# Second layer of a two-layer transformer block: the maxima's remainder on GpSimd, another order of the transposed scores, and a later copy of the attention outputs

## What is computed

```python
q, k, v = heads(xn @ Wq.T) * 8 ** -0.5, heads(xn @ Wk.T), heads(xn @ Wv.T)
sim = where(key > query, -max, q @ k.T)
e = exp(sim - max(sim, axis=-1))            # the maximum of each query's row
attn = (e @ v) / (sum(e) + 1e-8) @ Wo.T
moe = sum over 8 experts of (silu(xn @ wg) * (xn @ wu)) @ wd    # 128 -> 512 -> 128
x = x + attn + moe
```

## Time and profile before

| | us |
|---|---|
| three runs | 1370.39, 1373.32, 1380.13 (median 1373.32) |
| the profiled execution's time | 1372.09 |
| its span, first to last instruction | 1370.4 |
| PE busy | 1304.3 (95%) |
| DVE busy | 1017.8 (74%) |
| ACT busy | 823.6 (60%) |
| POOL busy | 738.1 (54%) |

### The profile page before, as it was taken

One profiled execution on the slowest core, in us unless ns is written; L12 is line 12 of the kernel. 1 busy time (PEld: TensorE's weight loads), 2 busy tenths in 40 slices (PEclk: granted clock), 3 DMA queues, 4 the chain that ended last, 5 costly groups with the idle time before them and its releaser, 6 DMA issues. The chain is left out here.

```text
span 1370.4 us, 23500 instructions
## 1 busy us (share of the span) xinstructions
PE 1304.3 (95%) x8328; PEld 779.8 (57%) x8328; DVE 1017.8 (74%) x2369; ACT 823.6 (60%) x1235; POOL 738.1 (54%) x859
## 2 busy tenths in 40 slices
PE   8999999999999969999999999999999999999996
PEld 5444545554455435665665665665665666666664
DVE  4676777777777647877887887787787788788764
ACT  2456666666766736666666666666566566566561
POOL 6154464664655535565655655655655654655551
PEclk9899999999999989999999999999999999999999
DMA  5222232423433311112112111111110110100002
GB/s 190 63 93 72 93 119 93 136 89 125 135 107 105 120 54 33 36 43 65 51 51 65 52 51 36 35 51 32 39 51 30 40 52 29 41 28 30 18 16 85
DMA packets 57683, 90.94 MB, mean 66 GB/s; under 512 B 12087, under 2 KB 23356, under 8 KB 57566
## 3 DMA queue, kind: packets, MB, share of 16 engines
q1 hardware_dynamic: 56414, 88.91, 20.5%
q10 hardware_dynamic: 1152, 0.52, 0.1%
HBM read 43.75 MB, written 44.53 MB: 64 GB/s over the span
## 5 line engine op out<-in xcount | busy, mean ns | idle before, releaser
L1261 POOL TENSOR_TENSOR a_h_lo<-a_h,a_h_hi 128x512 fp32r<-128x512 f32 x256 | 328.8, 1285 | 153.8 <-ACT a_h_hi L1333 153.2
L192 POOL TENSOR_SCALAR_AFFINE_SELECT E<-E 128x256 f32<-128x256 f32 (+1 forms) x384 | 195.1, 511 | 350.8 <-ACT E L1340 209.0
L701 DVE TENSOR_REDUCE mx<-bank_pair 128x2 f32<-128x1024 f32 (+3 forms) x264 | 209.5, 818 | 110.6 <-PE bank_pair L949 109.1
L1415 DVE SCALAR_TENSOR_TENSOR a_h<-a_h,bank_pair 128x512 f32<-128x512 f32 x256 | 175.2, 685 | 144.5 <-ACT a_h L1329 144.4
L1333 ACT ACTIVATE a_h_hi<-a_h 128x512 fp32r<-128x512 f32 x256 | 161.6, 631 | 128.4 <-DVE a_h L1421 125.6
L1340 ACT ACTIVATE E<-bank_pair 128x1024 f32<-128x1024 f32 (+1 forms) x192 | 169.6, 883 | 114.9 <-PE bank_pair L140 114.9
L168 DVE CUSTOM_DVE_ANT_0 bank_pair<-bank_pair,mask 128x512 f32<-128x512 f32 x496 | 230.6, 517 | 0.0
L133 PE MATMUL bank_pair<-st 24*128 24x512 f32 (+3 forms) x1024 | 200.1, 387 | 17.2 <-ACT E L789 3.5
L789 ACT ACTIVATE E<-bank_pair 128x1024 f32<-128x1024 f32 (+1 forms) x192 | 168.3, 878 | 70.3 <-PE bank_pair L140 68.8
L1421 DVE TENSOR_TENSOR a_h<-a_h,bank 128x512 f32<-128x512 f32 x256 | 176.1, 688 | 27.4 <-DVE a_h L1415 0.9
L1329 ACT ACTIVATE a_h<-bank_pair 128x512 f32<-128x512 f32 x256 | 151.1, 590 | 74.8 <-PE bank_pair L1556 73.4
(11 more groups left out here) (201 smaller groups left out, 2331.3 us busy)
## 6 DMA issues: line engine op xcount, KB each, us to landing
st<-stack_d SPq DMA_DIRECT2D x256, 96.0 KB
o_d<-O SPq DMA_DIRECT2D x64, 256.0 KB, 2.1
stack_d<-l_q_k_hi SPq DMA_DIRECT2D x56, 256.0 KB, 3.1
stack_d<-l_q_k_lo SPq DMA_DIRECT2D x28, 256.0 KB, 3.4
st<-ms SPq DMA_DIRECT2D x128, 8.0 KB
wst<-wg_in SPq DMA_DIRECT2D x8, 256.0 KB, 2.9
wst<-wu_in SPq DMA_DIRECT2D x8, 256.0 KB, 3.2
wst<-wd_in SPq DMA_DIRECT2D x8, 256.0 KB, 3.7
```

The lines of the kernel that those rows point to most:

```text
L192: return nc.gpsimd.affine_select(out=part, in_=part, compare_op=ALU.is_ge, fill=0.0, base=0, pattern=pattern, channel_multiplier=-1)
L701: ins = nc.vector.tensor_reduce(out, pair[:, :, col:col + width(kb)], AX.X, ALU.max)
L1261: nc.gpsimd.tensor_tensor(h_lo[:, q % RH, :], h[:, q % RH, :], h_hi[:, q % RH, :].bitcast(F32), ALU.subtract).then_inc(h_lo_ready, 1)
L1415: nc.vector.scalar_tensor_tensor(hq, hq, 1.0, g_bank[:, :], ALU.add, ALU.mult).then_inc(silu_ready, 1)
```

## The change

Five edits, all in `attend_moe`:

1. **The maxima's remainder.** `negations` goes. VectorE now writes the rounded maxima, not negated, with a `tensor_reduce` over an axis of length one (`tops`, slot 5). GpSimd subtracts that from the maxima (`rest_of_maxima`, 128x16 numbers, at the head of slot 6). The sign is put in by `copy_mrow` with `scale=-1.0`.
2. **Order of the transposed scores.** 0, 1, 3, 4, 5, 2 instead of 0 to 5 (`KEY_ORDER`), for the matmuls, the exponentials and the zeros.
3. **The copy of the outputs.** `outputs(g - 1)` moves on ScalarE from behind `hi` of slot 3 to slot 7, between `copy_mrow` and `hi`.
4. **Late units.** ("A", k) for k from 1 to 7 moves from quad 4k+1 to 4k+2; V of batch 6 goes to quad 5 and V of batch 7 to quad 9.
5. **SyncE.** The inverse's spreading load (`load_share`) is issued ahead of the outputs' store, not behind it.

```diff
+KEY_ORDER = (0, 1, 3, 4, 5, 2)
...
-LATE = {0: ("X", 6), 1: ("A", 0), 2: ("X", 7), 3: ("Q", 6), 4: ("K", 6), 5: ("A", 1), 6: ("V", 6), 7: ("Q", 7), 8: ("K", 7), 9: ("A", 2),
-        10: ("V", 7), 13: ("A", 3), 17: ("A", 4), 21: ("A", 5), 25: ("A", 6), 29: ("A", 7)}
+LATE = {0: ("X", 6), 1: ("A", 0), 2: ("X", 7), 3: ("Q", 6), 4: ("K", 6), 5: ("V", 6), 6: ("A", 1), 7: ("Q", 7), 8: ("K", 7), 9: ("V", 7),
+        10: ("A", 2), 14: ("A", 3), 18: ("A", 4), 22: ("A", 5), 26: ("A", 6), 30: ("A", 7)}
...
                 if due[0] == "A":
                     store_rden(due[1])
+                if due[0] == "A":
+                    load_share(due[1])
                 if g > 0:
                     sp.wait_ge(O_copied, g)
                     store_outputs(sp, o_d, O, g - 1, o_out[(g - 1) % 2])
-                if due[0] == "A":
-                    load_share(due[1])
                 if coming[0] == "A" and coming[1] > 0:
                     load_attention(coming[1])
...
+            def rest_of_maxima(g):
+                pool.wait_ge(top_ready, g)
+                nc.gpsimd.tensor_tensor(neg_part(nm, 1), mx[:, g % 2, :, :], neg_part(nm, 0).bitcast(F32), ALU.subtract).then_inc(nm_ready, 1)
...
                 for n in range(NC):
+                    if odd and n == 2 and g + 1 < QUADS:
+                        rest_of_maxima(g + 1)
                     if odd and n < 3:
                         causal(g, 3 + n)
...
-                nc.scalar.activation(ms[:, g % 2, :], M_bank[0:MAXIMA, :], ACT.Copy).then_inc(mrow_ready, 1)
+                nc.scalar.activation(ms[:, g % 2, :], M_bank[0:MAXIMA, :], ACT.Copy, scale=-1.0).then_inc(mrow_ready, 1)
...
                     if odd and n == NC - 1 and g + 1 < QUADS:
                         copy_mrow(g + 1)
+                    if odd and n == NC - 1 and g > 0:
+                        outputs(g - 1)
                     hi(NC * i + n)
...
-                    if not odd and n == NC - 1 and g > 0:
-                        outputs(g - 1)
...
-            def negations(g):
+            def tops(g):
                 dve.wait_ge(S_used, SCORES * g)
                 if g > 1:
                     dve.wait_ge(mT_ready, g - 1)
-                negate(nc, nm, mx, g).then_inc(neg_ready, 1)
-                dve.wait_ge(neg_ready, g)
-                negate_rest(nc, nm, mx, g).then_inc(nm_ready, 1)
+                nc.vector.tensor_reduce(neg_part(nm, 0), mx[:, g % 2, :, :].unsqueeze(3), AX.X, ALU.max).then_inc(top_ready, 1)
```

More of the change, by code:

```diff
@@ L1165, in attend_moe @@
         mrow_in = sem("mrow_in")
-        neg_ready, nm_ready, mT_ready, mrow_ready = (sem(n) for n in ("neg_ready", "nm_ready", "mT_ready", "mrow_ready"))
+        top_ready, nm_ready, mT_ready, mrow_ready = (sem(n) for n in ("top_ready", "nm_ready", "mT_ready", "mrow_ready"))
         S_ready, S_used, T_ready, exp_done = sem("S_ready"), sem("S_used"), sem("T_ready"), sem("exp_done")
@@ L1267, in split, with causal @@
                                         ALU.subtract).then_inc(w_lo_ready, 1)
-            def causal(g, n):
-                pool.wait_ge(exp_done, UNITS_A_QUAD * g + n + 1)
+            def causal(g, m):
+                n = KEY_ORDER[m]
+                pool.wait_ge(exp_done, UNITS_A_QUAD * g + m + 1)
                 keep_causal(nc, E[:, (PLANES * g + n // 3) % SLOTS_E, :], n % 3).then_inc(masked, 1)
+            def rest_of_maxima(g):
+                pool.wait_ge(top_ready, g)
+                nc.gpsimd.tensor_tensor(neg_part(nm, 1), mx[:, g % 2, :, :], neg_part(nm, 0).bitcast(F32), ALU.subtract).then_inc(nm_ready, 1)
             def rest_of_late(kind, b):
@@ L1333, in hi, with exp @@
                 nc.scalar.activation(h_hi[:, q % RH, :], h[:, q % RH, :], ACT.Copy).then_inc(h_hi_ready, 1)
-            def exp(g, n):
+            def exp(g, m):
+                n = KEY_ORDER[m]
                 at_col, w, pair = EXP_AT[n % 3], EXP_WIDTH[n % 3], PLANES * g + n // 3
-                act.wait_ge(T_ready, UNITS_A_QUAD * g + n + 1)
+                act.wait_ge(T_ready, UNITS_A_QUAD * g + m + 1)
                 if n % 3 == 0 and pair >= SLOTS_E:
@@ L1468, in _ @@
                     if more and odd and n == 1:
-                        negations(g + 1)
+                        tops(g + 1)
                     if odd and n == 2 and coming[0] == "A":
@@ L1495, in scores_and_keys @@
                 score_blocks = UNITS[n % 3] if more else []
-                key_blocks = UNITS[m % 3] if here else []
+                key_unit = KEY_ORDER[m] if here else 0
+                key_blocks = UNITS[key_unit % 3] if here else []
                 for k in range(2):
@@ L1506, in scores_and_keys @@
                         if k < len(key_blocks):
-                            ins = keys_by_queries(nc, T_banks[:, r, :], stacks[g % STACKS], r, m // 3, key_blocks[k])
+                            ins = keys_by_queries(nc, T_banks[:, r, :], stacks[g % STACKS], r, key_unit // 3, key_blocks[k])
                             if r == HALVES - 1 and k == len(key_blocks) - 1:
```

## The result

| | before | after |
|---|---|---|
| median, us | 1372.88 (4 runs) | 1400.31 (4 runs) |
| lowest to highest | 1370.39 to 1380.13 | 1398.22 to 1405.07 |
| ratio | | 1.0197, 95% interval 1.0162 to 1.0232 |
| profiled execution, span | 1372.09, 1370.4 | 1399.45, 1397.7 |
| mean granted clock of TensorE | 0.980 | 0.961 |

The account below looks back on a forecast made before the run. TensorE's queue was taken to set the time. From 1372.1 us, gains of 28.2 came off and 1 (SyncE's queue), 30.5 (wait at `invert`) and 7 (clock) were added: 1382 us, range 1361 to 1402.

Parts of the forecast that it names:

- The wait at `invert`: Slot 6, seven quads: VectorE waits for `den`, so TensorE stands 4.65 us each time, 30.5 us in all.
- The clock: TensorE's clock falls behind two of the seven stalls, 3.3 us a fall, taken as 7 us; bounds 0 and 23.
- I take 1 us in all: SyncE at the quad's end: the moved copy delays the maxima's rows, 1 us in all, bounds 0 and 6.
- The gain of 0.90 us a quad: Remainder and order: 0.36 + 0.10 + 0.34 + 0.10 us a quad, 28.2 us in all.
- slot 3 becomes like slot 1: Slot 3, new order: from scores to `down` 0.77 falls to 0.43 us, 0.34 us less a quad.
- VectorE must run earlier too. It can: Slots 4 and 5: with the copy gone from ahead of slot 4's `tanh`, VectorE's work moves up by 0.35 us.
- The remainder: Slot 5: the reduction runs unblocked at L180's price, 1.2 us less on VectorE, of which TensorE gains 0.36 + 0.10 a quad.
- the cover: GpSimd, slot 6: the subtraction is ready about 1 us before TensorE wants it in slot 7, so it costs nothing.
- (a): Rival: TensorE's clock falls at every stall, 23 us for the falls, 1398 us; chance 0.22.
- (b): Rival: VectorE eats the order's gain, only 14 us are won, 1397 us; chance 0.13.
- (c): Rival: more is won, 1.4 us a quad and no fall of the clock, 1358 us; chance 0.10.
- (d): Rival: the wait at `invert` does not bite and the change only gains, 1345 us; chance 0.05.

Follow-up runs that it names:

- f1: The changed kernel with the inversion of ("A", 1 to 7) moved to slot 1 of the quad LATE names: 1360.19 us, ratio to before 0.9903.
- f3: The changed kernel with both repairs, the inversion a quad later and the parts' stores ahead of SyncE's wait: 1343.36 us, ratio to before 0.9785.
- f2: The changed kernel with SyncE issuing the Q and K parts' stores ahead of its wait for the outputs' copy: 1387.74 us, ratio to before 1.0115.
- e7: The changed kernel with 18 more matmuls, output unread, on TensorE in slot 7 of quads 13, 17, 21, 25 and 29: 1393.61 us, ratio to before 1.0170.
- g3: f3 with VectorE's `add_acc` of slots 2 and 6 behind the slot's maxima, not ahead of them: 1338.39 us, ratio to before 0.9749.
- g1: f3 without the new order of the transposed scores: 1350.48 us, ratio to before 0.9831.
- f4: The kernel before with only the remainder on GpSimd and the new order, outputs' copy still in slot 3: 1356.60 us, ratio to before 0.9879.
- g4: f3 without the new order and without the remainder on GpSimd: 1370.13 us, ratio to before 0.9987.
- e5: The kernel before with only the new order of the transposed scores, outputs' copy still in slot 3: 1385.59 us, ratio to before 1.0114.

## Why the prediction was right, and where it was not

**Direction and mechanism.** The wait at `invert` was named with its place, its count and its length, and it is what makes the kernel slower: without it the change gains 1% (f1). The number was less good. The measured 1400 us lies inside the range, 2 us from its end, and 18 us above the forecast, which by itself meant "same"; same had the largest chance (0.48), slower 0.41. By terms the prediction had -28.2 + 1 + 30.5 + 7 = 10.3 us. The runs give about -29.5 + 12.6 + 30.1 + 15 = 28 us, an estimate from f3, f2, TensorE's idle time and e7, against 27.4 measured. So two terms were too small, edit 3's and the clock's, and two were right. By steps:

- **The wait at `invert`** (edits 4 and 5). Forecast 4.65 us of TensorE standing; measured 4.64 at quad 17, and VectorE idle 33.0 / 7 = 4.7 us. In all 30.5 us were forecast, with about 1 us less in quads 5 and 9, and TensorE idled 30.1. The chain held in each link: with `den` landing 2.2 us after its issue, behind the store, and not 2.4. Right.
- **The clock.** The term was two falls of 3.3 us, 7 us. It fell in all the seven places (0.71 to 0.86 as the mean clock of the 10.3 us from TensorE's next start), and behind the two of the next item (0.70 and 0.76). A fall cost 2.2 us in e7's traces, which makes 15 us for seven, an estimate; by e7's medians it is 1.3 us. The step that failed is the count: five of the stalls are longer than the idle 3.9 us behind which the clock had fallen, and the 3.1 us that "did nothing" were the chance of one execution, as the twelve traces above show. Here rule and trace agree: what the Trainium skill says of the gate ("TensorE: Matmul & The Clock Gate", its first part) was weighed as able to make any of the seven fall, and it made all of them.
- **"I take 1 us in all"** (edit 3, on SyncE's queue at the quad's end). The text asked only who waits for the maxima's rows behind the parts' stores, and that was right: 0.7 us. It did not ask who waits for the parts' stores themselves. ScalarE does, in quads 4 and 8, and that is 12.6 us with the clock's falls behind these waits (f2), above the item's bound of 6. This is the largest miss.
- **The gain of 0.90 us a quad.** 29.5 us measured in f3 against 28.2. The sum was right by luck, for its parts were not; errors of 0.24 and 0.20 us a quad cancelled. Slot 6 gave 0.35 as forecast (0.36). Slot 7 gave 0.20 and not 0.10. Slot 3 gave 0.10 and not 0.34: "slot 3 becomes like slot 1" overlooked that the second half of slot 3's scores already waited for VectorE (g3), whose `add_acc` stands ahead of slot 2's maxima. Slot 5 gave 0.20 and not 0.10: 0.07 is there without the new order (g1), 0.12 comes with it. These parts add up to 0.85 us a quad; the rest of the 29.5 us was not traced.
- **"VectorE must run earlier too. It can"** (edit 2). The reading of the earlier trace rows, that the copy of the outputs held slot 4's `tanh`, is borne out where the order is changed: 0.9% between f4 and f3. In the kernel before it was not: moving the copy alone won nothing (g4). But the 0.44 us were booked on the order, and with the copy where it was the order alone costs 15 us. That L180 could be blocked too was left out; it begins only 0.15 us ahead of `lo`.
- **The remainder.** The reduction took over L180's place and was not blocked, at 0.17 us, although it too begins 0.07 us behind `lo`, in each of 30 quads; this is what the Trainium skill says ("SBUF — State Buffer", section "Who interferes with whom"), and the trace agrees. GpSimd's piece costs 0.22 us; the cover was enough but once (1.3 us).

**Rivals.** (a), the clock falling each time at 1398 us, came nearest to the number. Its mechanism is what happened, but its price of 23 us for the falls is about 8 too high, and it lacks the two waits for the parts; that these nearly cancel is luck. (b) came true only in kernels without the remainder or with the copy in slot 3. (c) and (d) did not come.

## What to carry to other kernels

When an instruction moves later, list everything that is queued behind its signal on other engines, transfers included, and for each of them ask who waits for it and where that waiter stands in its own order; here one late copy made an inversion and two readings of a tile wait, and repairing two lines turned 2% slower into 2% faster. An edit that speeds one engine should be weighed with the state of the engine it alternates with: the same order of matmuls cost 1.1% or won 0.5%, depending on what VectorE and ScalarE did beside it. And a stall of TensorE should be priced with the slower clock behind it: every one of 3.5 to 4.6 us in the change was followed by it, at about half of its length again (2.2 us behind 4.6).

## What the runs showed of the hardware that was not expected

- A `tensor_scalar` over 16 numbers a partition in SBUF took 0.216 us on average before and 1.211 us in e5, until a GpSimd subtraction beside it ended, with nothing of it changed but the moment: it began 0.15 us ahead of the subtraction before, and 0.07 us behind its start in e5. A `tensor_reduce` on the same numbers took 0.170 us on average in the change, though it began inside such a subtraction in each of 30 quads.
- Both instructions of the pair can be blocked one after the other by one backlog: 1.24 and 1.20 us in one quad of e5.
- The clock fell in the middle of a wait (0.71 between 998.0 and 1000.5 us) and was 0.50 up to 1005; the price was 2.2 us in the profiled executions, and 18 matmuls whose output nobody reads took it away there.
- The same idling of 3.2 us behind the second layer left the clock at 1.00 in 2 of 14 traces and was followed by 0.50 in 12.
